# Layer 1: the softmax division moves from the attention into the feed-forward, and the attention's value products are issued two steps at a time

## The reference, cut to what matters

```
q, k, v = (proj(wq), proj(wk), proj(wv))          # 16 heads of 32
q, k = apply_rope(q, k, sin, cos)
att = einsum('bhqd,bhkd->bhqk', q, k) * (1.0 / sqrt(HD))
att = softmax(att, axis=-1)
y = einsum('bhqk,bhkd->bhqd', att, v)
s = y.transpose(0, 2, 1, 3).reshape(b, t, c) @ wo.T
g = silu(qlinear(silu(gate) * up, down))          # gate, up, down: quantised weights
x = x + s * g
```

## Time and profile before

| what | us |
|---|---|
| median of 3 runs (3283.95 to 3290.11) | 3285.88 |
| profiled execution, its own time | 3295.37 |
| its span, first to last instruction | 3292.0 |
| PE busy | 2926.6 (89%) |
| DVE busy | 1971.3 (60%) |
| POOL busy | 1324.0 (40%) |
| ACT busy | 1277.8 (39%) |
| mean granted TensorE clock, share of full | 0.949 |

### The profile page before, as it was taken

One profiled execution on the slowest core, in us unless ns is written; L12 is line 12 of the kernel. 1 busy time (PEld: TensorE's weight loads), 2 busy tenths in 40 slices (PEclk: granted clock), 3 DMA queues, 4 the chain that ended last, 5 costly groups with the idle time before them and its releaser, 6 DMA issues. The chain is left out here.

```text
span 3292.0 us, 56401 instructions
## 1 busy us (share of the span) xinstructions
PE 2926.6 (89%) x19876; PEld 2109.3 (64%) x19876; DVE 1971.3 (60%) x2924; ACT 1277.8 (39%) x1987; POOL 1324.0 (40%) x971
## 2 busy tenths in 40 slices
PE   5999999199999984799999999999999659999999
PEld 4888888078888873555555555555554248888887
DVE  4666665767777753676666666666666234444444
ACT  2111111066666651254544555455554412222222
POOL 1111010322333320377777777777777812112111
PEclk9999999599999996799999999999999979999999
DMA  2100000312222223111211111121111042212211
GB/s 83 33 32 32 32 32 20 118 52 96 96 90 82 99 74 113 52 54 63 65 59 59 64 58 59 58 65 58 59 59 33 13 184 74 70 64 72 72 64 51
DMA packets 97053, 215.00 MB, mean 65 GB/s; under 512 B 11408, under 2 KB 27792, under 8 KB 96400
## 3 DMA queue, kind: packets, MB, share of 16 engines
q1 hardware_dynamic: 95472, 210.14, 19.1%
q10 hardware_dynamic: 1440, 2.76, 0.2%
HBM read 162.54 MB, written 50.33 MB: 65 GB/s over the span
## 5 line engine op out<-in xcount | busy, mean ns | idle before, releaser
L1134 DVE TENSOR_REDUCE l_attn_maxima<-l_attn_ps_max 128x2 f32<-128x1024 f32 x512 | 618.6, 1208 | 229.7 <-PE l_attn_ps_max L1188 229.6
L1101 POOL TENSOR_TENSOR l_attn_summed<-l_attn_summed,l_attn_probs 128x1024 f32<-128x1024 f32 x256 | 600.4, 2379 | 132.6 <-ACT l_attn_probs L1052 132.5
L1052 ACT ACTIVATE l_attn_probs<-l_attn_ps_sc 128x1024 f32<-128x1024 f32 x512 | 496.7, 1022 | 274.1 <-PE l_attn_ps_sc L1177 271.5
L1101 POOL TENSOR_TENSOR l_attn_summed<-l_attn_probs 128x1024 f32<-128x1024 f32 x128 | 302.0, 2381 | 304.7 <-ACT l_attn_probs L1052 304.7
L70 PE MATMUL l_ffn_ps_gu<-l_ffn_w_gu,l_ffn_xt 128*128 128x512 f32 (+1 forms) x1536 | 345.0, 377 | 46.8 <-DMA l_ffn_xt<-xt_chunks 46.8
L61 PE MATMUL l_attn_ps_prep<-l_attn_wqkv_hi,l_attn_xt 128*128 (+1 forms) x1024 | 301.5, 378 | 74.7 <-DMA l_attn_xt<-xt_chunks 55.2
L70 PEld LDWEIGHTS l_ffn_ps_gu<-l_ffn_w_gu,l_ffn_xt 128*128 128x128 f32 x1536 | 279.1, 189 | 87.2 <-DMA l_ffn_xt<-xt_chunks 48.3
L1367 POOL TENSOR_TENSOR l_ffn_mixed<-l_ffn_gate,l_ffn_up 128x512 f32<-128x512 f32 (+1 forms) x96 | 115.1, 1199 | 521.8 <-DVE l_ffn_up L1416 473.5
L1188 PE MATMUL l_attn_ps_max<-l_attn_qk_hi 32*128 32x512 f32 x1024 | 252.6, 488 | 71.4 <-DVE l_attn_maxima L1134 71.3
L1188 PEld LDWEIGHTS l_attn_ps_max<-l_attn_qk_hi 32*128 32x128 f32 x1024 | 98.7, 189 | 281.7 <-DVE l_attn_maxima L1134 204.8
L1198 PE MATMUL l_attn_ps_y<-l_attn_probs,l_attn_v 128*32 128x512 f32 x2048 | 278.0, 616 | 1.1 <-ACT l_attn_probs L1052 1.1
(11 more groups left out here) (235 smaller groups left out, 6215.1 us busy)
## 6 DMA issues: line engine op xcount, KB each, us to landing
l_attn_xt<-xt_chunks SPq DMA_DIRECT2D x128, 512.0 KB, 3.3
xt_chunks<-l_ffn_xt SPq DMA_DIRECT2D x32, 512.0 KB, 4.6
l_ffn_xt<-xt_chunks SPq DMA_DIRECT2D x32, 512.0 KB, 3.3
l_attn_xin<-in_x SPq DMA_DIRECT2D x32, 256.0 KB, 2.7
s<-l_attn_s_sb SPq DMA_DIRECT2D x32, 256.0 KB, 2.0
l_ffn_xa<-in_x SPq DMA_DIRECT2D x32, 256.0 KB, 2.7
l_ffn_xb<-in_x SPq DMA_DIRECT2D x32, 256.0 KB, 2.9
l_ffn_s_sb<-s SPq DMA_DIRECT2D x32, 256.0 KB, 4.0
```

What stands on the lines that cost most here:

```text
L1052: act.activation(probs[kt % RING][:, hs, :], ps_sc[:, hs, :], ACT.Exp, scale=ATT_SCALE).then_inc(exp_done, 1)
L1101: pool.tensor_tensor(total[:, hs, :], old[:, hs, :], probs[kt % RING][:, hs, :], ALU.add).then_inc(added, 1)
L1134: dve.tensor_reduce(maxima[b][:, j, PAIR * hp:PAIR * hp + PAIR, half:half + 1], ps_max[:, :, :], AX.X, ALU.max).then_inc(max_read, 1)
```

## The change

Four edits go together.

- The attention stores values and denominators apart: ACT copies both from PSUM, SP stores both, and the inversions (DVE) and products (POOL) are gone from it. `den_chunks` is a new tensor in HBM of the size of `yt_chunks`.
- The feed-forward loads `den` beside `yt` for chunk t+2 in tick t, inverts it on the DVE in four pieces (two after cut 1 and two after cut 2 of tick t), multiplies on the POOL at the end of tick t, and ACT takes `yt_hi` from the product. All engines start at tick -2.
- `xt` of the attention has four buffers instead of two, and SP's stores are placed between the loads.
- The PE's order: in even steps scores, maxima, the value products of the two steps before, second maxima, event. In odd steps three of the four score sets, maxima, the last set, projection, second maxima, and no value product.

```diff
@@ layer1_attention, SP
+            def load(m, c):
+                if live(m, NT):
+                    b = c % XTS
+                    need(sp, proj_done, CPB * m + c - XTS + 1)
...
+            def tick(t, p):
+                load(t, 0)
+                store(t - 2, 0, y_copied, y_sb, yt_out)
+                load(t, 1)
+                load(t, 2)
+                load(t, 3)
+                store(t - 2, 0, den_read, den_sb, den_out)
...
+                store(t - 2, 1, y_copied, y_sb, yt_out)
+                load(t, 7)
+                store(t - 2, 1, den_read, den_sb, den_out)
@@ layer1_attention, POOL and DVE
-                            pool.tensor_tensor(y_sb[qb][:, :], y_sb[qb][:, :], inv_den[:, :], ALU.mult).then_inc(y_ready, 1)
-                            dve.reciprocal(inv_den[:, cols], inv_den[:, cols]).then_inc(inverted, 1)
@@ layer1_attention, PE
+                    first = (0, 1, 2) if s % 2 else (0, 1, 2, 3)
                     if live(m, NT):
-                        scores(m, parity(p, 0 if s < CPB else 1), qb, kt)
+                        scores(*mine, first)
                     if todo:
                         maximum(*todo[0])
+                    if live(m, NT) and s % 2:
+                        scores(*mine, (3,))
+                    if s % 2 == 0:
+                        for back in (2, 1):
+                            m, qb, kt = quad(t, s - back) if s else quad(t - 1, STEPS - back)
+                            if live(m, NT):
+                                pv(m, parity(p, 0 if s <= CPB else 1), qb, kt)
+                        for a in todo[1:]:
+                            maximum(*a)
                     if event(t, s):
                         prepare(t, p, s)
@@ layer1_ffn, SP
                     need(sp, gu_done, 2 * N * (c - 1))
...
+                    sp.dma_start(yt[b][:, :, :], yt_in[c]).then_inc(yt_den_ld[b], 16)
+                    need(sp, y_scaled, c - 1)
+                    sp.dma_start(den[b][:, :, :], den_in[c]).then_inc(yt_den_ld[b], 16)
@@ layer1_ffn, POOL, ACT, DVE
+                c, b = t + 2, p
+                if live(c, CHUNKS):
+                    need(pool, inverted, GROUPS * (c + 1))
+                    pool.tensor_tensor(yt[b][:, :, :], yt[b][:, :, :], den[b][:, :, :], ALU.mult).then_inc(y_scaled, 1)
...
-                    need(act, yt_ld[b], 8 * (c - b) + 16)
+                    need(act, y_scaled, c + 1)
...
+                    ci, bi = t + 2, p
+                    if live(ci, CHUNKS) and n:
+                        need(dve, yt_den_ld[bi], 16 * (ci - bi) + 32)
+                        for g in (2 * n - 2, 2 * n - 1):
+                            dve.reciprocal(den[bi][:, g, :], den[bi][:, g, :]).then_inc(inverted, 1)
```

More of the change, by code:

```diff
@@ L859, in layer1_attention @@
     RING = 4
-    PIECES = 4
+    XTS = 4
     PAIR = HPG // 2
@@ L915, in _ @@
                     dve.tensor_tensor(w_lo[:, k, :, :], raw[:, k, :, :], fp32(w_hi[:, k, :, :]), ALU.subtract)
-        xt = two("xt", [P, 2, KD, P], F32R)
+        xt = [sb(f"xt{i}", [P, 2, KD, P], F32R) for i in range(XTS)]
         x_tok = [sb(f"x_tok{i}", [P, 2, P]) for i in range(4)]
@@ L1011, in _ @@
         def _(sp):
-            def tick(t, p):
-                for c in range(CPB):
-                    if live(t, NT):
-                        b = c % 2
-                        src = sp.snap(t // GROUPS * CPB + c) if not isinstance(t, int) else t // GROUPS * CPB + c
-                        need(sp, proj_done, CPB * t + c - 1)
-                        sp.dma_start(fp32(xt[b][:, :, :, :]).rearrange("p h k n -> p (h k n)"), xt_in[src]).then_inc(xt_ld[b], 16)
-                for qb in range(QB):
-                    if live(t - 2, NT):
-                        store(t - 2, qb)
@@ new lines, in store @@
+            def store(m, qb, ready, tile, out):
+                if live(m, NT):
+                    four = CPB // QB
+                    at, grp = m // GROUPS * CPB + qb * four, m % GROUPS
+                    if not isinstance(m, int):
+                        at, grp = sp.snap(at), sp.snap(grp)
+                    need(sp, ready, QB * m + qb + 1)
+                    sp.dma_start(out[bass.ds(at, four), :, bass.ds(grp, 1), :].rearrange("c p a n -> p c (a n)"),
+                                 tile[qb][:, :].rearrange("p (c n) -> p c n", n=P)).then_inc(y_den_stored[qb], 16)
@@ L1315, in layer1_ffn @@
         xt = two("xt", [P, 2, KD, P], F32R)
-        yt = two("yt", [P, GROUPS, P])
+        yt, den = two("yt", [P, GROUPS, P]), two("den", [P, GROUPS, P])
         yt_hi, yt_lo = two("yt_hi", [P, GROUPS, P], F32R), two("yt_lo", [P, GROUPS, P], F32R)
@@ L1326, in layer1_ffn @@
         ps_down = [ps(f"ps_down{i}", [P, DIM]) for i in range(2)]
-        xt_ld, yt_ld, x1_ld, stored = ([sem(f"{n}{i}") for i in range(2)] for n in ("xt_ld", "yt_ld", "x1_ld", "stored"))
+        xt_ld, yt_den_ld, x1_ld, stored = ([sem(f"{n}{i}") for i in range(2)] for n in ("xt_ld", "yt_den_ld", "x1_ld", "stored"))
+        inverted, y_scaled = sem("inverted"), sem("y_scaled")
         yt_hi_ready, yt_lo_ready = sem("yt_hi_ready"), sem("yt_lo_ready")
@@ L1354, in tick @@
                     sp.dma_start(out_t[c], res[b][:, :]).then_inc(stored[b], 16)
-            ticks(sp, -2, 4, CHUNKS - 2, CHUNKS + 1, tick)
+            ticks(sp, *sched, tick)
             for b in range(2):
```

85 lines of the change are left out of this document (35 added, 50 removed).

## The result

| | before | after |
|---|---|---|
| median, us | 3287.99 (3283.95 to 3294.42, 4 runs) | 3426.11 (3410.52 to 3432.87, 4 runs) |
| ratio | | 1.0411, 95% interval 1.037 to 1.0453 |
| profiled execution, its own time | 3295.37 | 3432.87 |
| its span | 3292.0 | 3431.1 |
| mean granted TensorE clock | 0.949 | 0.939 |

The forecast was 3441 and the time is 3426. The two stages tell more than the sum: the feed-forward lost 133.4 us (forecast 189), and the attention, which was to win 34, lost 5.7. Two errors of 40 to 56 us cancel in part.

A forecast was written before the change was run, and what follows sets the result against it. The PE was read as nearly always busy, so its waits decide. Feed-forward +180, start +9 and attention -34 gave +155 on the profiled 3295.4, so 3450, or 3441 us timed; the 8-in-10 range was 3388 to 3490.

The forecast's parts named there:

- The load is issued too late for where the DVE wants it, and the PE stops: Feed-forward: DVE waits for den with ht_lo queued behind, stopping the PE's down product in 30 ticks, +180 us with clock.
- Size of the stall, 3.7: Feed-forward down product: the PE resumes at 2918.8 instead of 2915.07, a stall of 3.7 us per tick.
- Size of the clock's loss, 2.3: Feed-forward chunks: the granted clock falls after each stall, costing 2.3 us more; 6.0 us per tick together.
- The start, +9: Feed-forward's start: a longer chain to the first gate scaling stalls the PE some 7 us, plus 2 us of clock.
- The waits for x go, -51 with their clock and -5 at the end: Attention: 13 load waits go, -34 us, with clock losses of -17; inversions and product at the very end go, -5.
- The maxima wait, +29: Attention: the even maxima product waits 0.8 to 1.0 us for the DVE's reduce; pairs lengthen, +29 us in all.
- The border's credit, -7: Attention, where the loop jumps back: the new maxima wait lies inside the existing gap, -7 us.
- The sum: Whole kernel: feed-forward +180, its start +9, attention -34, together +155 us; timed runs 3441 us.
- (1) the load hidden: Feed-forward: the wait for den stays in the shadow and the kernel gets faster, 3261 us; chance 0.05.
- (2) the clock doesn't fall: Feed-forward: the stall of 3.7 us is there but the clock stays up, +84, 3370 us; chance 0.11.
- (3) the load lands later: Feed-forward: den lands later, 4.5 us of stall and 3.0 of clock, +200, 3486 us or more; chance 0.14.

The follow-up runs named there:

- e1: Changed kernel with SP issuing the feed-forward's yt and den loads ahead of the xt load that waits for projections, from chunk 2 on: 3292.5 us, ratio 1.0005.
- e2: Changed kernel with the den load left late and all four DVE inversions of a tick behind its last ht_lo: 3304.3 us, ratio 1.0032.
- e3: Changed kernel with the PE's attention order of the kernel before, all else changed: 3360.1 us, ratio 1.0205.
- e9: Kernel before with only four attention input buffers and SP's stores placed between the loads, division left in the attention: 3232.8 us, ratio 0.9818.
- e8: Changed kernel with second maxima reduced before rotation, yt and den loads issued first, first gate scaled earlier at the feed-forward's start: 3229.0 us, ratio 0.9807.
- e13: e8 with the PE's attention loop written out, so without its six jumps back: 3206.6 us, ratio 0.9748.

## Why the prediction was right, and where terms of its sum were not

- **The load is issued too late for where the DVE wants it, and the PE stops:** right, in 29 rows of 2.5 us on average, and one more in tick 0 behind a gate, 2.8. e1 and e2 take it away from both sides.
- **Size of the stall, 3.7:** it is 2.5. In the chunk at 3000 the 17th down matmul would have started at 3003.77 and did at 3006.44, so 2.67 from start to start. Three parts make the difference: `den` was issued and landed 0.6 us earlier against the down product than x1's load in the earlier trace rows; `res` takes 0.54 to the next start and not 0.90, and no product of the POOL runs beside it now; and the rest is the semaphore. A chunk is 23.05 us long and not 25.
- **Size of the clock's loss, 2.3:** the block lost 123.6 us beyond its start, 4.12 for each of 30 ticks. Less 2.5 this is 1.6. From 2724 to 3400 the granted clock is 0.94, which alone is some 40 us, 1.4 for each tick. I had taken 2.3 from the earlier trace rows, nearer to the longer stall; a stall of 2.5 us lies at the shorter one of 2.38, whose 1.4 would have fitted. No run shows the 3.0 that the upper bound took for an engine full of matmuls. Together 6.0 x 30 = 180 became 124.
- **The start, +9:** 9.8, by the chain of steps as written (stop of 7.26 us, forecast 7).
- **The waits for x go, -51 with their clock and -5 at the end:** right, -60.6 by e3, against -56. The kernel before has seven stalls on these loads of 3.8 to 4.25 us, the first ahead of 1483.74, where six were counted, which is 2.6 of the 4.6 us. (Its PE is busy for 89 to 93 of each 100 us from 1600 to 2400, not 91 to 93.) e9 has the gain without the end's: -54.7.
- **The maxima wait, +29:** the mechanism is right to the hundredth (0.88, from 2.30 between the two maxima products), the size is not. The turn pairs cost 0.23 to 0.31 more, as worked out, but den pairs 0.49, and the pairs with the maxima's transposes 0.47 (9.38 against 8.91), which I had never worked out and counted as turn pairs. In all a tick without the border is 78.05 us against e3's 74.98, so 3.1 and not 2.0 for each tick: 45 by the forecast's own count of 14.5, not 29.
- **The border's credit, -7:** the step was right and its price failed in sign. The new wait does hide in the gap: no maxima product behind a gap waits. What was put at nothing is that the gap grows (from 1.76 to 2.33), that the odd step's value product, which ran ahead of the gap, now stands behind it, and that with the clock at half there the two take 3.58 us and not 1.85. The border pair is 14.0 us, 4.3 above its neighbour; in e3 it is 11.7, 2.4 above, and the clock falls behind two of its six gaps, where it falls behind all six in the changed kernel. That is 6 x 1.93, +12 where the forecast took 7 off. Counted in the two traces, the 66.3 are 37 for 12 ticks of 3.1, 12 for the borders, 8 in the first three ticks, and 10 in the last tick and the end, which stay open.
- **The sum:** the feed-forward was forecast 56 us too dear and the attention 40 too cheap. The total of +155 against +138 owes its look to that, and that is luck: with the attention's -34 as forecast the time would have been 3386, just below the range of 3388 to 3490. The mechanism of the feed-forward, the larger part, is no luck.
- **Rivals:** (1) the load hidden: no. (2) the clock doesn't fall: no, though it fell less. (3) the load lands later: no, 3.8 against 4.1. By the estimate from the Trainium skill, "DMA: Bandwidth & Descriptors", section "Anatomy of one DMA", it would have been 2.6; that section is on DMAs that GpSimd issues, and these are SyncE's, third in a row. Here too the trace disagrees, by 1.2 us. For x1's load, with none ahead of it, it agrees within 0.2 (2.5, median 2.8).

## What to carry to other kernels

An in-order engine that waits for a load holds up all that stands behind it: put what consumes a late load last on its queue, or issue the load ahead of one that has to wait for something else. When work is taken from between two uses of the same PSUM tile, work out how long the reader of that tile takes, for every kind of step and not for one of them. And the worth of an edit depends on its neighbours: the same division was free on a VectorE with time to spare and made a kernel 45 us slower once TensorE had been packed around it.

## What was not expected of the hardware

- TensorE's gap after a loop's jump: 1.76 us in the earlier trace rows, 2.33 in the same place after. The granted clock was at half for what follows behind all six in the changed kernel and behind three of six in e8, where it fell behind gaps of 2.0 to 2.6 us and stayed full behind gaps of 2.1 to 2.4. Without the six jumps the pairs there are 18 us shorter in all and the median 22 (e13).
- `res`, a DVE operation of 128x512, took 0.98 us in the earlier trace rows, where it lay beside a product on the POOL, and 0.63 after, where none was. In e2 the two overlap by 0.24 to 0.45 us and `res` takes 0.79 to 0.99, the longer the more they overlap. No run changed the POOL's product alone.
- Waits of up to 0.4 us, 104 of them, left the clock at full from 1420 to 2380 in e13; behind stalls of 2.1 to 2.8 us in the feed-forward it came down in 23 of 29 cases (the product at 3007.93 has 1.00, behind a stall of 2.50).
